# A graph-network kernel on one core: transposed z and score products in the first attention pass, one-source one-hots and PSUM weights in both

## The chip, the core and the metric

The kernel runs on one core of a Trainium2 chip. The time is device microseconds from the start to the end of one execution. Engines: PE (matrix products; PEld is its weight load), DVE (vector), ACT (scalar and activation), POOL (GpSimd, which here issues the indirect gathers) and SP (which issues other DMAs).

## The reference

Four graph layers one after another over 6250 nodes with 128 features and 100,000 edges, each followed by a residual addition and a layer norm. The change touches the two attention layers. The first (4 heads of 32) scores an edge by `att`, per head, on a leaky sum:

```python
e = jax.nn.leaky_relu(x_l[src] + x_r[dst], NEG_SLOPE)      # (edges, 4, 32)
logits = jnp.einsum('ehc,hc->eh', e, att)
p = jnp.exp(logits - m[dst])                               # m: maximum per target
alpha = p / (segment_sum(p, dst)[dst] + 1e-16)
out = segment_sum(x_l[src] * alpha[:, :, None], dst)
```

The third layer (8 heads of 16) scores by the dot product of a query and a key row; the rest is the same with the roles of source and target exchanged:

```python
att = jnp.sum(Qh * Kh, axis=-1)                            # (edges, 8)
alpha = segment_softmax(att, row, num_nodes)
out = segment_sum(Vh * alpha[:, :, None], row)
```

## The kernel before

The edges are sorted by target and by source, and padded with one edge per node to 832 tiles of 128 positions. Five passes gather over these tiles: the first attention pass (`l0`, up to 3592 us of the trace), a scalar-score pass (`l1`), the second attention pass (`l2`, `dot` is true, from 5172 us), and two sum passes (`l3a`, `l3b`). Each pass is a loop over 208 groups of G = 4 tiles. It ends with a barrier, and node steps lie between the passes, so that a pass overlaps with nothing else.

In a pass, POOL does only `gather_rows` (L938): four indirect gathers a group of 128 rows each, into a ring of 8 groups (`RING`). It goes on when the group that last used the buffer is done with it; in the attention passes that is `val_done` of seven groups before. SP loads the window of node rows of each tile (L1051) and the run masks (L1053), four and six groups ahead. ACT's queue loads the slot rows and stores the partial sums.

The engines run a software pipeline in the order in which the code lists it; step k of each loop works on several groups:
- PE: transpose of the scores of group k-2 (L1069), transpose of the weights of k-3 (L1074), z of k, sums of k-4 (L1093). In the first pass z is, for each tile, the one-hot `sel_t` as weights with the window rows streamed (L1084), plus the identity with the gathered rows (L1086). An f32 product is two instructions; so z is 16 and the sums are 8.
- ACT: relu of z of k (L1116, only `l0`), copy of the weights of k-3 from PSUM into `val` (L1122), copy of the sums of k-4 to SBUF (L1127), exp of k-2 (L1133).
- DVE: `sel_t` of k+1 (L1145), prefix scan of k-2 (L1151), leaky of k-1 (L1163; in `l2` the product of z and the rows, L1158), top scan of k-2 (L1167), `prod` = z times att of k-1 (L1172, only `l0`), `sel` of k-3 (L1178), diff of k-2 (L1184), the value multiplication `val` of k-3 (L1188), the reduction of `prod` to the scores of k-1 (L1195) and a small copy (L1199).

The same two instructions in both passes have two SBUF sources of full size, `sel` and `val`; in `l0` there is `prod` besides. The sum passes build their one-hots from one tensor and one per-partition scalar a tile (L1410, L1412).

## Time and profile before

| what | us |
|---|---|
| median of 3 runs | 9392.61 (9376.02 to 9402.11) |
| the profiled execution | 9417.1 |
| its span | 9415.4 |
| mean granted clock of PE | 0.704 of full |

Busy over the whole span: POOL 5483 us (58%), PE 4862 us (52%), DVE 4576 us (49%), ACT 1853 us (20%). No engine is busy all the time, because the kernel has stages with different limits; the busy share of each has to be read stage by stage. The clock is the one that the chip grants to PE; it has two levels, 0.50 and 1.00, and a mean between them is a mixture. An idle time is written with what ended it; "issue" means that the profile shows nothing that the engine waited for, and "remote" that the releaser is not known. Ends of PE's instructions are modelled.

### The profile page before, as it was taken

How to read it: one execution, taken by the hardware profiler on the slowest of the kernel's cores; microseconds unless marked ns; L12 is line 12 of the kernel's file. 1: busy time of each engine (PE TensorE's matmuls, PEld its weight loads, DVE VectorE, ACT ScalarE, POOL GpSimd, SP SyncE). 2: the span in 40 equal slices, each digit the busy share in tenths (PEclk: the TensorE clock that was granted, in tenths of full speed). 3: DMA queues.
4: the chain of work that ended last, by engine and by line, in shares of the span. 5: the costliest groups of instructions: out<-in, count | busy, mean ns of one | idle time of the engine just before them, and what ended most of it. 6: DMA issues, size and time to landing. Idle time of an engine off the chain costs nothing. (4 is left out here: it accounts for less than half of the span.)

```text
span 9415.4 us, 112649 instructions
## 1 busy us (share of the span) xinstructions
PE 4861.8 (52%) x32998; PEld 3933.7 (42%) x32998; DVE 4576.4 (49%) x15755; ACT 1853.2 (20%) x4001; POOL 5483.4 (58%) x5311
## 2 busy tenths in 40 slices
PE   2367776777666663566665544544333334422322
PEld 2144444444555553556563444443233333322221
DVE  8866666663766666223233556555444443211113
ACT  0023333322222223111112111111222222211100
POOL 0235555553767673666663777775566665566664
PEclk9878888886888886555556767777666667655555
DMA  0011111114555552455553667665244443233332
GB/s 17 1 34 35 35 34 34 35 29 114 152 140 148 146 148 63 104 117 119 117 119 101 191 182 198 189 188 145 78 140 138 139 139 115 77 93 93 94 89 75
DMA packets 1304018, 990.43 MB, mean 105 GB/s; under 512 B 287713, under 2 KB 1192995, under 8 KB 1303411
## 3 DMA queue, kind: packets, MB, share of 16 engines
q0 software_dynamic: 183088, 352.33, 14.8%
q1 hardware_dynamic: 700995, 378.63, 14.4%
q10 hardware_dynamic: 419328, 252.26, 10.0%
q8 instruction: 273, 4.47, 0.2%
q14 instruction: 334, 2.74, 0.1%
HBM read 613.75 MB, written 368.79 MB: 104 GB/s over the span
## 5 line engine op out<-in xcount | busy, mean ns | idle before, releaser
L938 POOL DMA_INDIRECT l_rows<-tab,by_src x1664 | 1769.4, 1063 | 902.5 <-issue 480.2
L670 POOL DMA_INDIRECT sorted_dst<-pay,place_i x783 | 832.9, 1064 | 809.3 <-DVE place_i L618 590.6
L938 POOL DMA_INDIRECT l_rows<-tab,by_dst x832 | 945.4, 1136 | 520.5 <-issue 232.8
L938 POOL DMA_INDIRECT l3a_rows<-tab,by_dst x832 | 802.7, 965 | 440.3 <-issue 222.9
L938 POOL DMA_INDIRECT l3b_rows<-tab,by_dst x832 | 797.5, 958 | 421.6 <-issue 241.8
L1385 PE MATMUL l3b_ps_o<-l3b_rows,l3b_sel 128*128 128x128 f32 x1664 | 353.2, 390 | 837.3 <-issue 436.9
L1084 PE MATMUL l_ps_z<-l_win,l_sel_t 128*128 128x128 f32 x3328 | 732.0, 344 | 59.7 <-issue 19.1
L1385 PEld LDWEIGHTS l3b_ps_o<-l3b_rows,l3b_sel 128*128 128x128 f32 x1664 | 317.0, 289 | 873.9 <-issue 487.9
L1412 DVE TENSOR_SCALAR l3b_sel<-iota,by_dst 128x128 f32<-128x128 f16 x832 | 182.8, 296 | 1005.0 <-DMA lo_rows<-low_rows 827.4
L1084 PEld LDWEIGHTS l_ps_z<-l_win,l_sel_t 128*128 128x128 f32 x3328 | 586.7, 242 | 80.5 <-issue 44.3
L1409 DVE TENSOR_SCALAR l3a_kind<-iota,etype_at 128x256 f16<-128x256 f16 x832 | 244.7, 294 | 707.1 <-DMA l_win<-win 559.1
L1382 PE MATMUL l3a_ps_c<-l3a_kind,l3a_sel 128*128 128x256 f16 x832 | 186.1, 368 | 740.9 <-DVE l3a_sel L1412 526.5
L1093 PE MATMUL l_ps_o<-l_val,l_sel 128*128 128x132 f32 (+1 forms) x3328 | 567.4, 326 | 0.0
L1258 PE MATMUL l_ps_x<-l_win,l_sel_t 128*128 128x4 f32 x1664 | 364.6, 342 | 379.2 <-DVE l_e L1311 358.1
L1258 PEld LDWEIGHTS l_ps_x<-l_win,l_sel_t 128*128 128x128 f32 x1664 | 377.7, 332 | 398.8 <-DVE l_sel_t L1305 382.6
L1093 PEld LDWEIGHTS l_ps_o<-l_val,l_sel 128*128 128x128 f32 x3328 | 533.4, 238 | 0.3
L1265 PE MATMUL l_ps_o<-l_rows,l_sel 128*128 128x132 f32 x1664 | 438.0, 444 | 94.8 <-issue 94.3
L1127 ACT ACTIVATE l_sums<-l_ps_o 128x528 f32<-128x528 f32 (+1 forms) x416 | 257.1, 618 | 1126.6 <-remote 602.6
L1188 DVE TENSOR_TENSOR l_val<-l_rows,l_val 128x512 f32<-128x512 f32 x416 | 283.8, 682 | 318.7 <-ACT l_val L1122 232.5
L1315 DVE TENSOR_SCALAR l_sel<-iota,by_src,l_weight 128x128 f32<-128x128 f16 x832 | 247.7, 352 | 384.3 <-PE l_ps_o L1265 253.1
L1069 PE MATMUL l_ps_s<-ident,l_score 128*16 128x128 f32 (+1 forms) x416 | 127.3, 306 | 587.7 <-issue 310.5
L1265 PEld LDWEIGHTS l_ps_o<-l_rows,l_sel 128*128 128x128 f32 x1664 | 383.8, 333 | 101.2 <-issue 100.0
(412 smaller groups left out, 12542.6 us busy)
## 6 DMA issues: line engine op xcount, KB each, us to landing
parts<-l_sums ACTq DMA_DIRECT2D x416, 264.0 KB
l_win<-win SPq DMA_DIRECT2D x1664, 64.0 KB
parts<-l3a_sums SPq DMA_DIRECT2D x208, 512.0 KB
l_row<-slot_rows ACTq DMA_DIRECT2D x624, 128.0 KB
parts<-l_sums ACTq DMA_DIRECT2D x208, 272.0 KB
parts<-l3b_sums SPq DMA_DIRECT2D x208, 256.0 KB
low_bc<-lo_rows SPq DMA_DIRECT2D x194, 256.0 KB
l_rows<-tab,by_src POOLq DMA_INDIRECT x1664
```

Source lines behind the costliest of these rows:

```text
L670: pool.indirect_dma_start(sorted_dst, bass.IndirectOffsetOnAxis(ap=place_i[:, 4 * DST + s % 4, g:g + 1], axis=0), pay[:, col(s, g), :], No ...
L938: pool.indirect_dma_start(rows[:, q, g, :], None, table, bass.IndirectOffsetOnAxis(ap=index[:, k * G + g:k * G + g + 1], axis=0))\
L1084: mm = pe.matmul(ps_z[k % 2][:, g], sel_t[:, k % 2, g], win[:, b, g], start=True, stop=dot)
L1093: mm = pe.matmul(ps_o[j % 2][:, g // 2, g % 2 * w:(g % 2 + 1) * w], sel[:, j % 3, g], val[:, j % 2, g], start=True, stop=True)
L1127: act.activation(sums[:, j % OB].rearrange("p (i g) w -> p i (g w)", i=2), ps_o[j % 2][:, :, 0:2 * w], ACT.Copy).then_inc(sums_done, 1)
L1188: dve.tensor_tensor(val[:, j % 2, :, 0:D].rearrange("p g (h d) -> p g h d", h=heads), rows[:, j % RING, :, v0:].rearrange("p g (h d) -> p ...
L1258: mm = pe.matmul(ps_x[k % 2][:, g], sel_t[:, k % 2, g], win[:, b, g], start=True, stop=True)
L1265: mm = pe.matmul(ps_o[j % 2][:, g // 2, g % 2 * w:(g % 2 + 1) * w], sel[:, j % 2, g], rows[:, j % RING, g], start=True, stop=True)
L1315: return dve.tensor_scalar(sel[:, j % 2, g], c.iota16[:, 0:P], real_slot[:, at:at + 1], weight[:, j % 2, g:g + 1], ALU.is_equal, ALU.mult)
L1382: pe.matmul(ps_c[k % 2][:, g], sel16[:, k % 2, g], kind[:, k % 2, g], start=True, stop=True)
L1385: mm = pe.matmul(ps_o[k % 2][:, g], sel[:, k % 2, g], rows[:, k % RING, g], start=True, stop=True)
L1409: dve.tensor_single_scalar(kind[:, k % 2, g], c.iota16[:], types[:, at:at + 1], ALU.is_equal)
```

## The change

In the first attention pass z is formed transposed: the window rows and the gathered rows are the weights, and `sel_t` and the identity are streamed. After relu and leaky, the scores come from four products with `att_cols` (for each of the four tiles a 128 x 16 tile with att's heads in their columns), accumulated in PSUM; `prod`, its reduction and the transpose of the scores are gone there. `load_weights` builds `att_cols`. In both passes `sel` is built by four instructions with one tensor and one scalar, `val` reads the weights from PSUM (`ps_p`) and not from the copy in `val`, the weight transpose waits for `val_done` in place of `weight_done`, and ACT copies the weights before relu.

```diff
@@ load_weights
-                 (c.att[:], spread(w["L0_gnn_att"].rearrange("h c -> (h c)"))),
+                 (att_col[:], w["L0_gnn_att"].rearrange("h (c a) -> (h c) a", a=1)),
...
+            dve.memset(c.att_cols[:], 0.0).then_inc(rel_zero, 1)
...
+            flat = c.att_cols[:].rearrange("p g h -> p (g h)")
+            for h in range(heads):
+                own = slice(h * (D // heads), (h + 1) * (D // heads))
+                dve.tensor_copy(flat[own, h::G * heads + heads], att_col[own, 0:1].to_broadcast([D // heads, G]))
@@ attention_pass, PE
-                    pe.wait_ge(score_done, j + 1)
                     wait_count(pe, diff_done, j)
-                    pe.transpose(ps_s, score[:, j % 2], c.ident[:]).then_inc(score_ps, 1)
+                    if dot:
+                        pe.wait_ge(score_done, j + 1)
+                        pe.transpose(ps_s, score[:, j % 2], c.ident[:]).then_inc(score_ps, 1)
+                    else:
+                        pe.wait_ge(leaky_done, j + 1)
+                        for g in range(G):
+                            mm = pe.matmul(ps_s, c.att_cols[:, g], z[:, j % 2, g * P:(g + 1) * P],
+                                           start=g == 0, stop=g == G - 1)
+                        mm.then_inc(score_ps, 1)
...
-                    wait_count(pe, weight_done, j)
+                    wait_count(pe, val_done, j)
...
-                        mm = pe.matmul(ps_z[k % 2][:, g], sel_t[:, k % 2, g], win[:, b, g], start=True, stop=dot)
-                        if not dot:
-                            mm = pe.matmul(ps_z[k % 2][:, g], c.ident[:], rows[:, q, g], start=False, stop=True)
+                        if dot:
+                            mm = pe.matmul(ps_z[k % 2][:, g], sel_t[:, k % 2, g], win[:, b, g], start=True, stop=True)
+                        else:
+                            pe.matmul(ps_z[k % 2][:, g], win[:, b, g], sel_t[:, k % 2, g], start=True, stop=False)
+                            mm = pe.matmul(ps_z[k % 2][:, g], rows[:, q, g], c.ident[:], start=False, stop=True)
@@ attention_pass, ACT
-                if k < GROUPS and not dot:
-                    act.wait_ge(z_done, k + 1)
-                    wait_count(act, prod_done, k - 1)
-                    act.activation(z[:, k % 2], ps_z[k % 2].rearrange("p g d -> p (g d)"), ACT.Relu, scale=1.0 - LEAK)\
-                       .then_inc(relu_done, 1)
                 if 0 <= k - 3 < GROUPS:
...
                     act.activation(val[:, j % 2, :, D:w], ps_p, ACT.Copy).then_inc(weight_done, 1)
+                if k < GROUPS and not dot:
+                    act.wait_ge(z_done, k + 1)
+                    wait_count(act, score_ps, k - 1)
+                    act.activation(z[:, k % 2], ps_z[k % 2].rearrange("p g d -> p (g d)"), ACT.Relu, scale=1.0 - LEAK)\
+                       .then_inc(relu_done, 1)
@@ attention_pass, DVE
-                if 0 <= k - 1 < GROUPS and not dot:
-                    j = k - 1
-                    dve.wait_ge(leaky_done, j + 1)
-                    dve.tensor_tensor(prod[:, j % 2].rearrange("p (g d) -> p g d", g=G),
-                                      z[:, j % 2].rearrange("p (g d) -> p g d", g=G),
-                                      replicate(c.att[:], 1, G), ALU.mult).then_inc(prod_done, 1)
...
-                    dve.tensor_tensor(sel[:, j % 3], replicate(c.iota16[:, 0:P], 1, G),
-                                      replicate(slot[:, j * G:j * G + G], 2, P), ALU.is_equal)
+                    for g in range(G):
+                        t = j * G + g
+                        dve.tensor_single_scalar(sel[:, j % 3, g], c.iota16[:, 0:P], slot[:, t:t + 1], ALU.is_equal)
...
-                                      replicate(val[:, j % 2, :, D:w], 3, width), ALU.mult).then_inc(val_done, 1)
-                if 0 <= k - 1 < GROUPS:
+                                      replicate(ps_p, 3, width), ALU.mult).then_inc(val_done, 1)
+                if 0 <= k - 1 < GROUPS and dot:
```

## Rows read from the trace of the kernel before

**Rows 1.** Busy time by engine in the five gather passes, in order of time
```profile
...
core 0: us, PE busy (x) PEld busy (x) DVE busy (x) ACT busy (x) POOL busy (x), PEclk, DMA share, GB/s
2225.00:3592.00 1367.00, 855.77 (x5408) 769.53 (x5408) 932.79 (x2100) 304.09 (x833) 944.65 (x832) 0.83 0.55 144
3786.00:4991.00 1205.00, 741.72 (x3264) 716.36 (x3264) 361.86 (x1647) 150.82 (x405) 803.27 (x832) 0.50 0.53 117
5172.00:6530.00 1358.00, 682.79 (x3740) 590.09 (x3741) 792.87 (x1878) 215.04 (x624) 965.55 (x832) 0.72 0.66 189
6703.00:7892.00 1189.00, 452.18 (x2424) 384.72 (x2424) 482.95 (x2447) 297.79 (x400) 802.36 (x832) 0.64 0.45 135
8088.00:9265.00 1177.00, 348.50 (x1640) 312.46 (x1640) 179.87 (x819) 118.80 (x203) 797.46 (x832) 0.57 0.34 92
```

**Rows 2.** Waits of the first pass: total us, times, longest us
```profile
...
POOL l_rows L938 <- issue: 232.8, 758, 0.8
DVE l_val L1188 <- ACT l_val L1122: 229.1, 130, 6.6
...
ACT l_sums L1127 <- remote: 185.3, 65, 13.6
POOL l_rows L938 <- DVE l_val L1188: 160.2, 73, 9.7
...
PE l_ps_z L1084 <- DMA l_rows<-tab,by_dst: 5.3, 4, 1.7
```

**Rows 3.** Instruction groups, first pass, 2600 to 3200: busy us, mean ns, idle before
```profile
...
L938 POOL DMA_INDIRECT l_rows<-tab,by_dst x372 | 416.0, 1118 | 185.3 <-issue 101.6 <-DVE l_val L1188 83.7
...
L1195 DVE TENSOR_REDUCE l_score<-l_prod 128x16 f32<-128x512 f32 x90 | 61.1, 679 | 0.0
L1178 DVE TENSOR_TENSOR l_sel<-iota,by_dst 128x512 f32<-128x512 f16 x90 | 60.5, 672 | 0.0
L1172 DVE TENSOR_TENSOR l_prod<-l_z,att 128x512 f32<-128x512 f32 x90 | 58.8, 654 | 0.0
```

**Rows 4.** Instruction groups of the third pass, 5500 to 6100 us
```profile
...
L938 POOL DMA_INDIRECT l_rows<-tab,by_src x372 | 436.4, 1173 | 160.8 <-issue 111.0 <-DVE l_val L1188 49.7
```

**Rows 5.** Instruction groups of the fourth pass, 6800 to 7880 us
```profile
...
L938 POOL DMA_INDIRECT l3a_rows<-tab,by_dst x757 | 727.4, 961 | 355.0 <-issue 201.3 <-DMA l_win<-win 139.4 <-PE l3a_ps_o L1385 14.3
...
L1412 DVE TENSOR_SCALAR l3a_sel<-iota,by_dst 128x128 f32<-128x128 f16 x760 | 225.9, 297 | 0.0
```

**Rows 6.** Order of time, first pass, half clock: start us, duration us, engine
```profile
...
2925.26 0.95 POOL L938 DMA_INDIRECT l_rows<-tab,by_dst  x1 [0.30 <-issue]
2925.37 0.65 DVE L1163 SCALAR_TENSOR_TENSOR l_z<-l_ps_z,l_z 128x512 f32<-128x512 f32 x1
...
2926.07 0.80 PE L1084 MATMUL l_ps_z<-l_win,l_sel_t 128*128 128x128 f32 x2
2926.28 0.65 DVE L1172 TENSOR_TENSOR l_prod<-l_z,att 128x512 f32<-128x512 f32 x1
...
2926.51 1.86 POOL L938 DMA_INDIRECT l_rows<-tab,by_dst  x1 [0.30 <-issue]
...
2926.87 0.67 DVE L1178 TENSOR_TENSOR l_sel<-iota,by_dst 128x512 f32<-128x512 f16 x1
...
2929.64 1.97 PE L1093 MATMUL l_ps_o<-l_val,l_sel 128*128 128x132 f32 x8
```

**Rows 7.** Order of time, the next group, full clock
```profile
...
2932.71 0.46 PE L1084 MATMUL l_ps_z<-l_win,l_sel_t 128*128 128x128 f32 x2
...
2934.57 1.07 PE L1093 MATMUL l_ps_o<-l_val,l_sel 128*128 128x132 f32 x8
...
2938.14 0.61 ACT L1127 ACTIVATE l_sums<-l_ps_o 128x528 f32<-128x528 f32 x1 [2.70 <-remote]
```

**Rows 8.** Busy time in three us of each of these two groups
```profile
...
2926.00:2929.00 3.00, 3.00 (x14) 2.96 (x15) 1.74 (x5) 0.00 (x0) 2.39 (x3) 0.50 0.54 163
2933.00:2936.00 3.00, 2.63 (x24) 2.44 (x22) 2.49 (x6) 0.67 (x2) 2.39 (x3) 1.00 0.73 182
```

More of the change, by code:

```diff
@@ L678, in load_weights @@
         kit = Kit(nc, st)
-        att_cols = kit.sb("att_cols", [P, 2])
+        att_cols, att_col = kit.sb("att_cols", [P, 2]), kit.sb("att_col", [P, 1])
         kernel_t = kit.sb("kernel_t", [P, P])
@@ L768, in _ @@
             dve.wait_ge(turned, 4)
-            dve.wait_ge(rel_zero, 1)
+            dve.wait_ge(rel_zero, 2)
+            heads = 4
+            flat = c.att_cols[:].rearrange("p g h -> p (g h)")
+            for h in range(heads):
+                own = slice(h * (D // heads), (h + 1) * (D // heads))
+                dve.tensor_copy(flat[own, h::G * heads + heads], att_col[own, 0:1].to_broadcast([D // heads, G]))
             dve.tensor_copy(c.rel_w[:, 0], ps_rw[:, 0]).then_inc(copied, 1)
@@ L1957, in build @@
         c.w3 = kit.sb("w3", [P, 2, 3 * D])
-        c.gamma, c.beta, c.att = (kit.sb(n, [P, D]) for n in ("gamma", "beta", "att"))
+        c.gamma, c.beta = (kit.sb(n, [P, D]) for n in ("gamma", "beta"))
+        c.att_cols = kit.sb("att_heads", [P, G, G * 4])
         c.rel_w = kit.sb("rel_w", [P, 2, 2, D])
```

## The prediction

> **What bounds the kernel now.** I read first the table of the five gather passes [rows 1]: each is a loop of 208 groups with four gathers a group issued by POOL, 832 in all, and nothing of one pass overlaps the next. The change touches the first (from 2225 us) and the third (from 5172 us). The reader should compare the POOL column with the span. The three passes that are left alone take 1205, 1189 and 1177 us with POOL busy for 803, 802 and 797 us. The two that change take 1367 and 1358 us with POOL busy for 945 and 966 us, for the same 832 gathers. What the other engines do differs by far more (PE busy 856 us in the first pass and 349 us in the last) and moves the span less.
>
> Second, the waits of the first pass [rows 2]: between gathers POOL needs 233 us in small pieces of 0.3 us (issue), and 160 us for the value multiplication to free a buffer. PE waits for gathered rows only 5 us. So POOL is occupied for 945 + 233 = 1178 of 1367 us and the rest, 189 us, are stretches in which the ring of eight groups is full. The same subtraction with 0.3 us per gather (250 us) leaves 152, 137 and 130 us in the three other passes and 142 us in the third. The remainder hardly depends on what is computed; the POOL term does.
>
> Third, why a gather takes longer in the two passes. Its mean is 1118 and 1173 ns [rows 3, 4] against 961 ns [rows 5]. In the order of time [rows 6] a gather that starts at 2925.26 beside the leaky step, which reads PSUM and SBUF, takes 0.95 us; the one at 2926.51, beside prod (z and att, both SBUF) and then sel (iota and slot, both SBUF), takes 1.86 us and goes on till the end of the stretch of both. So a DVE instruction with two SBUF sources holds POOL's gather up; one with a PSUM source does not. The rows of the one-hots in the fourth pass, tensor against one scalar, stand beside gathers of 961 ns [rows 5]: those don't either.
>
> Fourth, PE. Its clock alternates between half (0.50, 1.2 GHz) and full (1.00, 2.4 GHz) [rows 8]. At half clock the eight z products take from 2926.07 to 2929.64, 3.57 us, and the sums 1.97 us; at full clock 1.86 and 1.07 us [rows 6, 7]. After the full-clock sums ACT still waits 2.70 us and the profile names no releaser; in the whole pass such waits are 185 us, up to 13.6 us long [rows 2, 7].
>
> **The change part by part.** *The two-source instructions go.* First pass: prod (654 ns), the reduction (679 ns) and the 672 ns sel go [rows 3]; the value multiplication keeps its size but reads the weights from PSUM; four one-source one-hots of about 297 ns come [rows 5]. DVE: -0.65 - 0.68 - 0.67 + 1.19 = -0.8 us a group, but it was busy only 933 of 1367 us, so this gives nothing by itself. POOL loses all its two-source partners but one, the top scan, which I take as harmless. Bound from the other passes: 945 - 803 = 142 down to 945 - 797 = 147 us saved, and nothing if the new one-hots hold gathers up too. I take 141 us, by the nearest pass in PE work. Third pass: 966 - 803 = 162 to 168 us, again nothing at the other end; I take 162 us.
>
> The Trainium skill, page "SBUF — State Buffer", section "Who interferes with whom", says that GpSimd shares one pair of ports with VectorE, and that a VectorE instruction with two SBUF inputs contends with GpSimd's reads; the lengthened gathers agree. It also says that tensor_scalar can enter a mode that uses both ports and then contends as well, which speaks against this change. By that rule the four one-hots could hold POOL for as long as the sel they replace, and the gain would be little or none; the fourth pass's 961 ns beside twelve such instructions a group does not show it [rows 5].
>
> *The one-hots in the third pass* cost DVE 4 x 0.297 - 0.65 = about 0.5 us a group, 112 us of busy time on top of 793 of 1358 us [rows 1]. They lie before diff, exp and the weight transpose. Hidden by POOL's pace it is nothing, wholly exposed 112 us; DVE stays below 80% of the new span, so I take 12 us.
>
> *PE in the first pass* loses one transpose of the scores and gains four products a group, each with a 16-column weight tile and 128 streamed columns. The nearest rows are the z products: 1.86/8 = 0.23 us at full and 3.57/8 = 0.45 us at half clock, so at most 0.9 and 1.8 us a group. Swapping weights and streamed operand of the z products leaves sixteen passes of 128 columns: nothing. At full clock PE needs 1.86 + 1.07 + 0.9 + 0.3 = 4.1 us, which lies under POOL's 4 x (0.965 + 0.30) = 5.06 us. At half clock it needs 3.57 + 1.97 + 1.8 + 0.3 = 7.6 us, and now a group at half clock takes 6.64 us from z to z [rows 6, 7]. A mean clock of 0.83 [rows 1] means 34% of the time at half clock: of some 1225 us that is 417 us or 55 groups, each 1.0 us longer, 55 us. The ring of eight groups and the earlier scores cover part: between 0 and 55, and below nothing if the earlier products keep the clock up; I take 20 us.
>
> *Order and waits.* The score products now wait for the leaky step instead of the reduction, an instruction earlier on DVE. ACT copies the weights before relu instead of after it, so that the value multiplication no longer waits for the z products: that wait is 229 us now, in 130 groups [rows 2]. It is a shorter way around the loop, but POOL sets the pace, so I count it only as what keeps PE's addition cheap. The weight transpose now waits for the value multiplication of the group before. Behind it on PE stand the z products and the sums, and ACT's relu waits for those. In the third pass PE has by then waited for a reduction that DVE does after that same multiplication: nothing. In the first it costs nothing as long as DVE runs ahead; if not, up to the 0.7 us of a value multiplication a group, 140 us. The loads of the start (a 128-value column in place of a broadcast, one memset, four small copies) are within 2 us and I take nothing.
>
> **Sum.** First pass -141 + 20 = -121 us; third pass -162 + 12 = -150 us; together -271 us. The profiled execution took 9417.1 us (span 9415.4), so 9146 us for it. The median of the runs shown is 9392.6 us, 24.5 us less, and the predicted time is 9392.6 - 271 = 9122 us.
>
> **The rivals.**
> *The first pass is PE-bound, the third gains.* All 55 us of PE and the 2.70 us waits stay, the way around the loop (z, sums, wait, ACT's sums and exp, weight transpose) remains the limit, and what POOL saves turns into waiting for the value multiplication. For it: PE waited for gathered rows 5 us only. Against: the remainder of 189 us is little more than the 130 to 152 us of passes with far lighter loops. First pass 0, third -150: 9243 us. Chance 0.16.
>
> *The one-hots hold POOL too* (the change does not do what it says; also the page's tensor_scalar rule). Then a gather stays at 1.12 to 1.17 us, and the extra DVE work is even: 9393 us, within 25. Against: 961 ns [rows 5]. Chance 0.07.
>
> *Slower: PE stays at half clock.* The second pass runs at 0.50 throughout although PE is busy 742 of 1205 us [rows 1]. If the first pass did the same, a group would need 7.6 us of PE, and adding the remainder common to all passes, 130/208 = 0.6 us, 8.2 us: 208 x 8.2 = 1706 us, +339. With -150 in the third, 9582 us. It decides as soon as a group of the first pass averages above 6.57 + 150/208 = 7.3 us. Against: the z products, which make the larger part of PE's work, are the same as now and had 0.83. Chance 0.06.
>
> *The stretches shrink as well.* The shorter way around the loop removes the excess of the first pass's remainder, 189 - 130 = about 60 us, and PE costs nothing: -141 - 60 - 162 = -363, 9030 us. Chance 0.13.
>
> **How the numbers follow.** The forecast, 9122 us, has 0.58; its own range is 9050 to 9220, by the ends of PE's 0 to 55 and DVE's 0 to 112 us. About 0.3% (28 us) is what a measurement of this kernel can tell from no change. The range that should hold the time 8 times in 10 takes in the forecast, most of the PE-bound case and the near side of the last one: 9040 to 9290. Faster: 0.58 + 0.16 + 0.13 = 0.87, less 0.02 for a PE-bound case that eats the third pass's gain: 0.85. Same: 0.08. Slower: 0.07.
>
> **What would show it.** The gathers of both passes at 0.95 to 0.97 us mean and POOL busy about 800 us in each; spans near 1245 and 1210 us. If the gathers shorten and the first pass's span does not, with POOL waiting for the value multiplication for over 250 us, PE or the loop was the bound. If the gathers stay above 1.1 us, the port argument is wrong. A mean clock of the first pass below 0.7 would make the slower case true. In the third pass DVE busy near 900 us is the price of the one-hots.

## The result, and the profile after

The changed kernel takes 9680.2 us (median of 4 runs, 9677.0 to 9696.1); the kernel before, run beside it, 9384.4 us. The ratio is 1.0333, with a 95% interval of 1.0311 to 1.0354: 296 us slower where the forecast was 271 us faster. The profiled execution took 9678.6 us, span 9676.8 us.

The table of the changed kernel by stretch, in the columns of [rows 1]; the first and the third line are the passes that change:

```profile
core 0: us, PE busy (x) PEld busy (x) DVE busy (x) ACT busy (x) POOL busy (x), PEclk, DMA share, GB/s
2202.00:3726.00 1524.00, 1019.34 (x6864) 909.80 (x6864) 722.54 (x2310) 328.01 (x833) 813.67 (x832) 0.82 0.49 130
3916.00:5121.00 1205.00, 740.52 (x3259) 715.26 (x3259) 360.29 (x1648) 150.66 (x405) 800.25 (x832) 0.50 0.53 117
5303.00:6790.00 1487.00, 758.21 (x3738) 658.86 (x3739) 829.95 (x2502) 210.51 (x624) 805.88 (x832) 0.69 0.60 172
6964.00:8156.00 1192.00, 448.71 (x2436) 383.06 (x2436) 481.85 (x2461) 298.88 (x403) 801.25 (x832) 0.65 0.45 135
8350.00:9527.00 1177.00, 341.21 (x1632) 305.94 (x1632) 179.23 (x814) 118.00 (x202) 794.83 (x832) 0.57 0.34 92
```

POOL's busy time fell as forecast, from 945 to 814 us and from 966 to 806 us, and yet the passes grew, from 1367 to 1524 us and from 1358 to 1487 us (157 + 129 = 286 of the 296 us). The three other passes are as they were. The gathers in the instruction groups of the changed kernel's first pass (busy us, mean ns | idle before):

```profile
L944 POOL DMA_INDIRECT l_rows<-tab,by_dst x832 | 814.0, 978 | 778.4 <-DVE l_val L1198 460.7 <-issue 219.8 <-POOLq L789 97.9
```

A gather takes 978 ns, near the 961 ns of [rows 5]. But POOL now waits 461 us for the value multiplication, where it waited 160 us [rows 2]. The waits of the changed kernel (total us, times, longest us), first pass:

```profile
DVE l_prefix L1166 <- remote: 474.3, 95, 8.3
POOL l_rows L944 <- DVE l_val L1198: 460.7, 122, 8.6
...
ACT l_sums L1142 <- remote: 257.2, 75, 6.7
ACT l_z L1136 <- remote: 236.7, 46, 26.4
```

and third pass:

```profile
ACT l_sums L1142 <- remote: 723.8, 89, 12.0
...
POOL l_rows L944 <- DVE l_val L1198: 421.9, 93, 9.3
```

"remote" means that the profile names no releaser. Each of these three instructions reads what PE has just put into PSUM: the scores, the sums, z. Two of them wait for a transfer as well (the sums for an earlier store, the scan for the run masks), but the trace's records of signals decide it: each of these waits ends at a signal that only PE gives, recorded over 1.5 us after the modelled end of the products that give it (for the sums at a median of 6.0 us, for the scores 6.0 us, for z 3.0 us). Whether the result or only its signal is late, they don't show. In the first pass ACT's wait for the sums grew from 185 [rows 2] to 257 us; the two others stood in the kernel before at:

```profile
DVE l_prefix L1151 <- remote: 59.1, 14, 11.8
ACT l_z L1116 <- remote: 150.6, 25, 10.5
```

The order of time of one such stretch, changed kernel (start us, duration us, engine, idle before):

```profile
3016.76 0.83 DVE L1189 TENSOR_SCALAR l_sel<-iota,by_dst 128x128 f32<-128x128 f16 x4
...
3017.43 0.39 PE L1101 MATMUL l_ps_z<-ident,l_rows 128*128 128x128 f32 x2
...
3017.66 1.07 PE L1108 MATMUL l_ps_o<-l_val,l_sel 128*128 128x132 f32 x8
...
3018.61 0.95 POOL L944 DMA_INDIRECT l_rows<-tab,by_dst  x1 [0.30 <-issue]
3018.65 1.05 PE L1080 MATMUL l_ps_s<-l_z,att_heads 128*16 128x128 f32 x8
...
3020.38 0.60 ACT L1136 ACTIVATE l_z<-l_ps_z 128x512 f32<-128x512 f32 x1 [4.31 <-remote]
3020.46 0.60 DVE L1160 TENSOR_SCALAR l_sel_t<-l_row,lane 128x512 f32<-128x512 f16 x1 [1.99 <-remote]
3020.52 4.14 SPq L1057 DMA_DIRECT2D l_win<-win  x4
...
3023.63 0.95 POOL L944 DMA_INDIRECT l_rows<-tab,by_dst  x1 [0.30 <-issue]
3024.70 0.61 ACT L1142 ACTIVATE l_sums<-l_ps_o 128x528 f32<-128x528 f32 x1 [3.71 <-remote]
...
3026.44 0.41 DVE L1166 TENSOR_TENSOR_SCAN l_prefix<-l_run,l_ps_s 16x128 f32<-16x128 f32 x1 [5.39 <-remote]
...
3029.59 0.95 POOL L944 DMA_INDIRECT l_rows<-tab,by_dst  x1 [5.02 <-DVE l_val L1198]
```

The z products end at 3017.82 as the profile models them, and the three instructions that wait for them on three engines (relu on ACT, the next `sel_t` on DVE, the next window on SP) start within 0.14 us of each other, from 3020.38 on. The sums' matmuls end at 3018.73, the score products at 3019.70; their readers start at 3024.70 and 3026.44. In between POOL issues gather after gather, one each 1.25 us. Then the ring is full, and POOL stands for 5.02 us until the loop that it ran ahead of has freed a buffer. The hold of the two-source instructions is gone, and a later result takes its place.

The passes that the change leaves alone have such waits too. In the last one POOL waits for the sums of PE alone (`sums_ps`); the label names an old transfer with the same signal number, but the signal that ends these waits is again PE's:

```profile
POOL l3b_rows L944 <- DMA lo_rows<-low_rows: 136.5, 36, 7.2
```

### The profile page after: what moved, and what is told of

It is laid out like the page before. It is cut to its first block and busy times, and to the rows that moved or that the text cites. A ratio compares the mean times of both kernels' runs of the same rounds, so it can differ in the third digit from the quotient of the medians.

```text
span 9676.8 us, 116192 instructions
## 1 busy us (share of the span) xinstructions
PE 5066.9 (52%) x34454; PEld 4125.2 (43%) x34454; DVE 4396.7 (45%) x16592; ACT 1870.6 (19%) x4001; POOL 5184.2 (54%) x5311
## 5 line engine op out<-in xcount | busy, mean ns | idle before, releaser
L944 POOL DMA_INDIRECT l_rows<-tab,by_src x1664 | 1606.6, 966 | 1194.8 <-issue 464.7
L944 POOL DMA_INDIRECT l_rows<-tab,by_dst x832 | 814.0, 978 | 778.4 <-DVE l_val L1198 460.7
L1166 DVE TENSOR_TENSOR_SCAN l_prefix<-l_run,l_ps_s 16x128 f32<-16x128 f32 (+1 forms) x416 | 169.6, 408 | 1095.4 <-remote 474.3
L1087 PE MATMUL l_ps_p<-ident,l_weight 16*128 16x16 f32 (+1 forms) x416 | 110.9, 267 | 1031.7 <-ACT l_weight L1148 768.1
L1108 PE MATMUL l_ps_o<-l_val,l_sel 128*128 128x132 f32 (+1 forms) x3328 | 600.0, 339 | 0.1
L1108 PEld LDWEIGHTS l_ps_o<-l_val,l_sel 128*128 128x128 f32 x3328 | 566.0, 251 | 0.5 <-DVE l_val L1198 0.3
L1087 PEld LDWEIGHTS l_ps_p<-ident,l_weight 16*128 16x128 f32 (+1 forms) x416 | 64.3, 155 | 1152.8 <-ACT l_weight L1148 824.3
L1392 PEld LDWEIGHTS l3a_ps_c<-l3a_kind,l3a_sel 128*128 128x128 f16 x832 | 90.9, 125 | 802.2 <-DVE l3a_sel L1422 563.9
L1100 PE MATMUL l_ps_z<-l_sel_t,l_win 128*128 128x128 f32 x1664 | 419.1, 342 | 20.4 <-DVE l_sel_t L1160 16.7
```

The costliest lines, as they stand in the source:

```text
L944: pool.indirect_dma_start(rows[:, q, g, :], None, table, bass.IndirectOffsetOnAxis(ap=index[:, k * G + g:k * G + g + 1], axis=0))\
L1087: pe.transpose(ps_p.rearrange("p g h -> p (g h)"), weight[:, j % 2], c.ident[0:hg, 0:hg])\
L1100: pe.matmul(ps_z[k % 2][:, g], win[:, b, g], sel_t[:, k % 2, g], start=True, stop=False)
L1108: mm = pe.matmul(ps_o[j % 2][:, g // 2, g % 2 * w:(g % 2 + 1) * w], sel[:, j % 3, g], val[:, j % 2, g], start=True, stop=True)
L1392: pe.matmul(ps_c[k % 2][:, g], sel16[:, k % 2, g], kind[:, k % 2, g], start=True, stop=True)
```

## The experiments

How a line is read below: *pass* is the time from the start of the first to the start of the last gather, slightly shorter than the stretches above; *gather* is the mean of one; *stalls* are POOL's pauses of over 0.8 us in the pass. For comparison, the kernel before: first pass 1337 us, gather 1.136 us, stalls 155 us; third pass 1330, 1.161, 118. The change: 1494, 0.978, 463; 1459, 0.969, 423. A pass repeats less well than the whole: the same code took 1376, 1377 and 1388 us in the third pass of three kernels, and 1501 and 1469 us in the first pass of one; differences under some 30 us in one pass are not read. All of these have the three other passes at 1170 to 1220 us; a second kind of session, with those at 1045 to 1059 us, comes after it.

### One hold at a time

*The change, with the one-hots of all four groups in one two-source instruction again.*

```
-                    for g in range(G):
-                        t = j * G + g
-                        dve.tensor_single_scalar(sel[:, j % 3, g], c.iota16[:, 0:P], slot[:, t:t + 1], ALU.is_equal)
+                    dve.tensor_tensor(sel[:, j % 3], replicate(c.iota16[:, 0:P], 1, G),
+                                      replicate(slot[:, j * G:j * G + G], 2, P), ALU.is_equal)
```

> The changed kernel with one part undone: sel is again one instruction with two SBUF sources. Theory A (the holds helped): the gathers that DVE held up gave PE's results room to come out; with sel back, a gather is about 1.05 us again on the mean, both passes shorten by 60 to 100 us against the changed kernel, about 9530 us in all. Theory B (plain cost): the third pass lost by the 0.5 us of the four one-hots and returns to 1358 us, the first pass stays at about 1520 us because its loss is PE's added products: about 9550 us, with the first pass unchanged as the mark that tells it from A.

Measured 9548.5 us, 1.0175 (1.0088 to 1.0263) of the kernel before (9380.1 us beside it). Passes 1449 (gather 1.030, stalls 365) and 1376 (1.005, 309). The first pass is 45 us shorter than the change's and not unchanged, which speaks for theory A, though for less than its 60.

*The change, with the value weights read from SBUF again.*

```
-                                      replicate(ps_p, 3, width), ALU.mult).then_inc(val_done, 1)
+                                      replicate(val[:, j % 2, :, D:w], 3, width), ALU.mult).then_inc(val_done, 1)
```

> The changed kernel with one part undone: the value multiplication reads the weights from their SBUF copy. Theory A (the holds helped): gathers lengthen by about 0.1 us, both passes shorten by 40 to 80 us, about 9560 us. Theory B (plain cost): the source of the weights costs nothing either way, 9680 us within 20.

Measured 9497.8 us, 1.0133 (1.0096 to 1.0169). Passes 1405 (1.049, 309) and 1359 (1.050, 249). Both put a source of hold back, both make gathers longer, and both make the kernel faster than the change, by 132 and 182 us (theory B had 9680 for the second).

*The kernel before, with the one-source one-hots alone* (the first diff, turned round).

> The kernel before with one part done: sel by four one-source instructions. Theory A (the holds helped): gathers near 1.02 us, both passes longer by 50 to 100 us with POOL's waits for the value multiplication up by as much as the gathers shrink and more, about 9540 us. Theory B (plain cost): 0.5 us of DVE a group matters only where DVE is in the loop: the third pass longer by 110 to 128 us, the first by less than 40, about 9510 us.

Measured 9558.1 us, 1.0186 (1.0066 to 1.0306). Passes 1501 (0.984, 467) and 1339 (1.047, 232). Its first pass in the table by stretch:

```profile
2211.00:3740.00 1529.00, 910.60 (x5371) 821.72 (x5371) 955.61 (x2698) 302.60 (x823) 818.43 (x832) 0.79 0.49 128
```

and in the list of waits:

```profile
POOL l_rows L938 <- DVE l_val L1189: 469.3, 134, 8.5
ACT l_sums L1127 <- remote: 392.3, 96, 7.9
DVE l_prefix L1151 <- remote: 258.8, 67, 6.2
```

This kernel has none of the new PE work, and its first pass is as long as the change's, with the same picture. So the loss does not need the added products. It does not follow that they are free: with the one-hots undone in the change, the first pass stayed at 1449 us, 112 above the kernel before. The third pass fits neither theory: it lost 95 us of POOL's busy time and is 9 us longer, where A had 50 to 100 and B 110 to 128.

*The kernel before, with the value weights read from PSUM alone*, and the weight transpose behind the value multiplication, as that needs.

```
-                    wait_count(pe, weight_done, j)
+                    wait_count(pe, val_done, j)
-                                      replicate(val[:, j % 2, :, D:w], 3, width), ALU.mult).then_inc(val_done, 1)
+                                      replicate(ps_p, 3, width), ALU.mult).then_inc(val_done, 1)
```

> The kernel before with one part done: the value multiplication reads the weights from PSUM, and the weight transpose waits for it. Theory A (the holds helped): both passes longer by 20 to 60 us, about 9460 us. Theory B (plain cost): no change in the third pass, where PE had waited for a later step anyway, and at most 20 us in the first: 9385 to 9405 us.

Measured 9488.1 us, 1.0111 (1.0024 to 1.0198). Passes 1349 (1.132, 171) and 1377 (1.008, 308). In the first pass nearly nothing changes, hold included; in the third the hold goes and the stalls come. Alone the two edits cost 178 and 108 us, together 286, about the whole change's 296. By pass they don't add up: 164 + 12 us in the first, where the change has 157, and 9 + 47 in the third, where it has 129.

*The same two again, in another session, beside the kernel before itself*, since two of these intervals are wide.

> The kernel before, profiled beside the others. If the light passes take about 1050 us: gathers of 1.15 to 1.2 us in the two attention passes, 4 x (1.17 + 0.25) = 5.7 us a group, about 1190 us a pass, no wait without a releaser, 8098 us. If they take 1170 us or more: as at first, 9390 us within 150.

> The kernel before with sel by four one-source instructions. Theory E, light passes of about 1050 us: POOL sets the pace, the gathers shorten by 0.08 to 0.14 us and each attention pass by 60 to 110 us: about 7940 us. Light passes of 1170 us or more: 1.5 to 2% slower than before, as b_sel_one.

> The kernel before with the value weights read from PSUM. Theory E, light passes of about 1050 us: gathers shorter by up to 0.15 us in the third pass, hardly in the first, together 50 to 130 us faster: about 8010 us. Light passes of 1170 us or more: about 1% slower than before, as b_val_psum.

Measured 1.0012 (0.9997 to 1.0026) for the kernel against itself, 1.0152 (1.0035 to 1.0269) for the one-hots (9547.7 against 9381.5 us) and 1.0096 (1.0079 to 1.0113) for the value weights. Passes 1469 and 1362, and 1345 and 1388. It repeats: + 166 and + 93 us. Beside the 1352 and 1338 us of the kernel before, run beside them, the one-hots cost the first pass 117 and the third 24 us, the value weights nothing in the first and 50 in the third.

*The new z and PE products alone*: the change with both of the first two diffs.

> The first pass's part alone: transposed z, scores from PE products, order and waits as in the changed kernel; sel with two SBUF sources and the value weights from their SBUF copy as in the kernel before. Theory A (the holds decide): prod's hold of 0.1 us a gather goes, so the first pass is 20 to 60 us longer; the third pass equals before within 15 us: about 9420 us. Theory B (plain cost of PE's products): the first pass longer by 100 us or more, 9490 us.

Measured 9631.9 us, 1.0123 (1.0024 to 1.0223) of a kernel before that took 9514.5 us beside it. First pass 1439 with stalls of only 162, but with POOL busy for 1034 us, more than the 945 before. In the order of time:

```profile
2909.26 0.65 DVE L1187 TENSOR_TENSOR l_sel<-iota,by_dst 128x512 f32<-128x512 f16 x1
2909.46 2.08 POOL L944 DMA_INDIRECT l_rows<-tab,by_dst  x1 [0.30 <-issue]
...
2910.04 0.67 DVE L1197 TENSOR_TENSOR l_val<-l_rows,l_val 128x512 f32<-128x512 f32 x1
```

The earlier weights let the value multiplication follow the one-hots at once, so one gather is held by both. This kernel is slow because of the hold, as the prediction's picture has it, and the price is the opposite of what the change pays. It isn't an isolated price of the products, as I had meant it to be: at this ratio it would take 9500 us beside a kernel before of 9384, theory B's number, but with POOL's hold for its reason.

Its third pass says something else. It differs from the kernel before by one wait alone, that of the weight transpose for the value multiplication; both two-source instructions are there. Yet POOL is busy 879 us instead of 966, its stalls are 262 instead of 118, and the pass takes 1376 us, 46 more, where at most 15 were expected (the slower session makes some 15 of them, by its other passes of 1218, 1199 and 1182 us). So the wait costs by itself, and less hold can also be the result of more stalls, and not only their cause.

### Pauses in POOL, and the ring

*The change, with POOL filling an unused tile after each group of four gathers.*

```
+                wait_count(pool, idled, k)
+                pool.memset(idle[:], 0.0).then_inc(idled, 1)
```

> The changed kernel, with a fill of a 128x768 scratch tile by POOL after each group's four gathers in the two attention passes, 0.7 to 0.8 us a group (128x128 fills start 0.14 us apart at the kernel's start). Theory A (any break in POOL's gathers lets PE's results out): both passes shorten by 80 to 130 us against the changed kernel, about 9470 us, although POOL does more. Theory C (what helped was something of DVE's two-source instructions other than the break): POOL's fill comes out of its waits for buffers, no pass is shorter: 9680 us or up to 50 more.

Measured 9613.4 us, 1.0104 (0.9971 to 1.0237) of 9514.5 us: about 220 us less than the change's 1.0333 would give (the low end of one interval and the high end of the other leave about 70 us; the two ratios come from two sessions), with more work. The fill in the groups of the whole span:

```profile
L1070 POOL MEMSET l_idle<- 128x768 f32 x416 | 314.5, 756 | 0.2
```

The third pass in the table by stretch, the fills among POOL's 968 us:

```profile
5337.00:6738.00 1401.00, 770.40 (x3727) 672.47 (x3727) 918.25 (x2498) 209.53 (x621) 968.28 (x1040) 0.68 0.64 183
```

315 us of idle work were put into POOL; the third pass is 1371 us (gather 0.976), 88 us less than the change's, and the first 1448 us, 46 us less, though even the kernel before, run beside it, took 1.4% longer than beside the change. The stalls fall to 259 and 191 us. The gathers are as many and as short; spaced, they cost less. The third pass meets theory A's 80 to 130 us, the first stays below them.

*Fewer groups ahead*: the ring keeps its eight buffers, but POOL may fill only six (first and second pass), five (third) and four (last two). Once in the change, once in the kernel before.

```
-    wait_count(pool, used, k - RING + 1)
+    wait_count(pool, used, k - ahead + 1)
```

> The changed kernel with POOL allowed fewer groups ahead, by a lower count in its wait alone: 6 in the first and second pass, 5 in the third, 4 in the two sum passes, where it was 8. Theory A (unbroken gathers delay PE's results): POOL stops after fewer gathers in a row, so each pass is shorter, the attention passes by 30 to 100 us each and the sum passes by 20 to 60. Theory D (the ring's depth is what carries the loop over the late results): fewer groups ahead make every pass longer, the attention passes by 50 us or more each.

> The kernel before with the same lower counts. Theory A (unbroken gathers delay PE's results): sum passes shorter by 20 to 60 us each, attention passes by 0 to 60, because DVE's holds break the gathers already: about 9300 us. Theory D (the ring's depth carries the loop): every pass longer, 9450 us or more.

Measured 1.0307 (1.0215 to 1.0398) and 0.9983 (0.9953 to 1.0012): in the change as slow as it is (passes 1527 and 1527), in the kernel before nothing (1379 and 1345), and the other passes stay at 1182 to 1220 us, as in the kernel with the fills beside them. Neither theory's number came: no pass got shorter, and only the change's third pass, 68 us longer (some 15 of them the session's), has what theory D gives. So a shorter lead, and with it a shorter unbroken run of gathers, takes nothing of the loss away.

### The same kernels in another kind of session

The next four kernels ran in a session where the kernel before took 8098.1 us, 14% less, with no edit of it.

> The kernel before with POOL's fill of a 128x768 scratch tile after each group's gathers in the two attention passes. Theory A (any break in POOL's gathers lets PE's results out, and DVE's holds, 0.7 us a group, do already what the fill does): little is left to gain, between 40 us faster and 60 us slower. If instead breaks simply add up, both passes shorten by 50 us or more each, down to the 1180 to 1200 us of the light passes.

> The changed kernel with the same length of fill cut in four, one of 128x192 after each gather. Theory A with the length of unbroken gathers as what counts: shorter pieces of POOL's work help as much or more than one break a group, 9470 us or less beside a kernel before of 9385. If the sum of the breaks or a break of at least some length counts: less than a_pause gave, 9550 to 9680 us.

(*b_pause*: the fill in the kernel before. *a_pause_each*: a fill of 192 values a partition after each single gather of the change.)

*Each gather brings 4 of a row's 128 values, as many gathers as before* (the text on record says what its output lacks):

```
+        pool.indirect_dma_start(rows[:, q, g, 0:4], None, table.rearrange("n (a b) -> (n a) b", b=4),
```

> The changed kernel in whose two attention passes each gather fetches 16 bytes a row in place of 512 or 1024 (the rest of the rows is a constant: the attention outputs are not the reference's). POOL issues as many gathers of 128 rows. If PE's late results come from the traffic of the gathers, both passes run at the pace of POOL, 5.1 us a group or 1070 to 1100 us each, and the waits without a named releaser nearly vanish. If they come from POOL's own work of issuing, the passes stay within 60 us of 1494 and 1459 us.

*One gather a group instead of four, in both attention passes of the change:*

```
-    for g in range(G):
-        pool.indirect_dma_start(rows[:, q, g, :], ...
+    pool.indirect_dma_start(rows[:, q, 0, :], ...
-                        pe.wait_ge(landed[q], landed_before[q] + 16 * G * (k // RING + 1))
+                        pe.wait_ge(landed[q], landed_before[q] + 16 * (k // RING + 1))
```

> The changed kernel in whose two attention passes only the first of the four gathers of a group is issued (the other rows are a constant: the attention outputs are not the reference's). It shows the loop's own pace. Theory A (POOL's gathers delay PE's results): 4.2 to 4.8 us a group, 870 to 1000 us a pass, and waits without a named releaser near nothing. Theory B (the loop is slow by itself, by PE's added work and its clock): the passes stay above 1350 us.

Measured, against 8098.1 us: the kernel before with fills 8363.8 us, 1.0322 (1.0282 to 1.0363), passes 1392 and 1348, POOL busy 1013 us with the gathers of the first and nowhere a stall, so that its fills are added work (266 us for some 315 of fills). The change with small fills 0.9949 (0.9928 to 0.9969), passes 1207 and 1235. The thin gathers 0.9640 (0.9612 to 0.9668), passes 1075 and 1112. One gather in four 0.8966 (0.8940 to 0.8992), passes 820 and 796 us: the loop without POOL's pace takes 3.9 us a group, less than the 4.2 to 4.8 expected. Nothing could be concluded on the loss, since it wasn't known whether it is there at all in such a session. So the unchanged change ran next, beside a repetition as a link to that session:

> The changed kernel once more. Theory E (two conditions): where the light passes take about 1050 us and no wait is without a releaser, POOL sets the pace and the two attention passes come down to 5.1 to 5.3 us a group, 1060 to 1100 us each, 3 to 4% faster than the kernel before beside it; where the light passes take 1170 us or more, it is 3% slower as at first. Theory B (plain cost of the change): slower by 1 to 3% in either.

> The changed kernel in whose two attention passes only the first of the four gathers of a group is issued (the other rows are a constant, so the attention outputs are not the reference's), once more. Where the light passes take about 1050 us: 820 and 796 us a pass as before. Where they take 1170 us or more: if POOL's gathers cause PE's late results, 820 to 900 us a pass and few waits without a releaser in the two; if something else causes them, 1000 us or more a pass, with those waits still there.

Measured 7797.6 us against 8098.5 us: 0.9627 (0.9608 to 0.9646). Here the same change is 301 us faster. The repetition gave 0.8974 (0.8952 to 0.8996), as before. The first and the third pass of the change there, in the table by stretch:

```profile
1623.00:2728.00 1105.00, 902.69 (x6872) 796.21 (x6872) 725.29 (x2315) 332.02 (x835) 825.29 (x837) 0.94 0.72 179
4102.00:5246.00 1144.00, 696.70 (x3752) 599.22 (x3752) 840.95 (x2507) 222.70 (x627) 867.07 (x838) 0.76 0.78 225
```

Its waits in the first pass:

```profile
POOL l_rows L944 <- issue: 245.1, 804, 0.3
...
PE l_ps_z L1100 <- DMA l_rows<-tab,by_dst: 181.6, 145, 3.7
```

and in the third:

```profile
DVE l_prod L1173 <- DMA l_rows<-tab,by_src: 252.2, 131, 5.8
```

POOL is busy in the first pass for about what it was in the other session (825 and 814 us; in the third 867 and 806), but no wait without a releaser is left in the first pass, POOL's waits for the value multiplication are gone (in the third pass 15 us are left, in pieces of 0.3 us), and now PE and DVE wait for gathered rows. POOL alone makes 825 + 245 = 1070 of the 1105 us. It is what the prediction described, but for one thing: the remainder is gone as well. In the kernel before, in the first kind of session, POOL's stalls are 155, 169, 118, 149 and 134 us in the five passes, in the change 463, 172, 423, 150 and 134; here POOL has no pause of over 0.8 us in any of the five. Its wait for PE in the last pass, 136.5 us above, has become:

```profile
POOL l3b_rows L944 <- PE l3b_ps_o L1395: 0.6, 2, 0.3
```

The two kinds of session part at one place. POOL's first indirect transfer comes at 392 us. The changed kernel in the first kind, its first 392 us and 966 us of the sort's scatters:

```profile
0.00:392.00 392.00, 109.74 (x1603) 82.09 (x1603) 363.12 (x1800) 3.67 (x5) 6.12 (x34) 1.00 0.04 11
534.00:1500.00 966.00, 686.24 (x7761) 454.16 (x7759) 598.86 (x2082) 299.52 (x480) 508.85 (x480) 0.83 0.14 34
```

The same kernel in the second kind, stretches of the same lengths:

```profile
0.00:392.00 392.00, 109.67 (x1603) 82.12 (x1603) 363.26 (x1801) 3.67 (x5) 6.12 (x34) 1.00 0.04 11
495.00:1461.00 966.00, 860.63 (x12301) 609.24 (x12302) 942.09 (x3287) 473.11 (x759) 742.65 (x733) 1.00 0.22 54
```

The first 392 us agree to a quarter of a microsecond in every column, so it isn't the speed at which the engines work by themselves. From the scatters on, the first kind gets 480 of them done in the time in which the second gets 733. Of the waits of that stretch in the first kind, one of ACT for PE's products again has no releaser:

```profile
ACT lo L412 <- remote: 287.4, 47, 9.6
```

*Fewer gathers in the first kind*: the kernel before, with one gather a group in the first pass alone.

> The kernel before in whose first attention pass only the first of the four gathers of a group is issued (the other rows are a constant, so the output is not the reference's); its third pass is as before. Light passes of 1170 us or more: if POOL's gathers cause PE's late results, the first pass runs at the loop's own pace of 4.6 us a group, 960 us, with few waits without a releaser; if not, it stays above 1200 us. Light passes of about 1050 us: the first pass 900 to 960 us, the third 1150 to 1200 us, its gathers 1.16 to 1.2 us.

Measured 8972.6 us, 0.9529 (0.9501 to 0.9557) of 9418.4 us. It fell in the first kind of session: from first to last gather its last pass takes 1175 us (the stretch of 1200 below takes in what follows), and its third 1325, as ever. The first and the last pass in the table by stretch:

```profile
2213.00:3140.00 927.00, 679.97 (x5268) 609.58 (x5268) 889.87 (x2043) 298.29 (x808) 198.85 (x208) 0.99 0.63 165
7650.00:8850.00 1200.00, 352.92 (x1664) 316.03 (x1664) 183.00 (x832) 121.58 (x208) 802.98 (x840) 0.57 0.35 92
```

and the waits of the first pass:

```profile
POOL l_rows L946 <- DVE l_val L1200: 716.9, 199, 11.3
ACT l_z L1128 <- PE l_ps_z L1098: 571.4, 203, 5.5
...
ACT l_sums L1139 <- PE l_ps_o L1105: 47.0, 200, 1.0
```

Every wait for PE names PE's own instruction again, and the one for the sums is never over 1.0 us (it was up to 13.6 us [rows 2]). The second pass of the same execution, untouched, keeps its late results (ACT's wait for its sums: 566 us without a releaser). So they go with POOL's gathers: gone at a quarter of them, there at four a group; rates in between were not tried. POOL's long wait here is what one gather a group leaves over.

## Why the prediction was wrong

*What sets POOL's busy time: right.* The gathers came to 978 and 969 ns and POOL to 814 and 806 us; 0.95 to 0.97 us and about 800 us were forecast. (One row was misread: the gather of 1.86 us does not go on till the end of prod and sel, 2927.54, but 0.83 us beyond it [rows 6].) Undoing either part brought some of the hold back, and each time the gather's mean rose (1.030 and 1.049 us).

*The one-hots hold POOL too: wrong, as given.* The Trainium skill, page "SBUF — State Buffer", section "Who interferes with whom", lets tensor_scalar take both ports in its 2-port modes. No hold as long as the instruction shows here; a small one does: the changed kernel's gathers with no DVE instruction beside them take 0.951 us, the 125 of the first pass beside the one-source `sel_t` alone 0.992 on the mean and up to 1.21 us. Its other rule, that two SBUF inputs of VectorE contend with GpSimd, agrees with the gather of 2.08 us above.

*PE's added products, + 20 us: neither confirmed nor refuted.* The one-hots without them gave 1501 and 1469 us for the first pass, the change 1494; no kernel has the products without either the hold or the late results. The clock was 0.82 (0.83 before), so the slower rival with PE at half clock did not occur; the loss has another mechanism, although that rival alone had the right direction.

*The one-hots in the third pass, + 12 us on DVE: too dear a price on DVE, and the wrong place.* DVE was busy for 830 us, not 900: four one-hots take 0.83 us together in the order of time, not 4 x 0.297.

*The wait of the weight transpose: counted at nothing in the third pass.* The value weights from PSUM lengthened that pass from 1330 to 1377 and 1388 us. There the hold's removal and the wait came together. The kernel with the new products alone has in that pass nothing but the wait, and took 1376 us, some 30 more than before if its slower session is allowed for (an estimate from its other passes). Beside one-source one-hots the same wait made 1359 against 1339 and 1362 us. So the wait's share lies between nothing and two thirds.

*The step that failed* is "The remainder hardly depends on what is computed; the POOL term does", and with it the terms of - 141 and - 162 us, which took the whole saving of POOL to be time of the pass. I had it from five passes whose remainders were 130 to 189 us (189 with 233 us for the pieces between gathers, but the others with 250; by the same 250 the first has 172). The remainder rose instead: POOL's stalls from 155 to 463 us and from 118 to 423 us. Spans of 1245 and 1210 us were forecast, 1524 and 1487 came.

Two readings went wrong in it. The first: in the first pass PE waited 5 us for gathered rows, so hardly anything waited for POOL, and POOL itself stood for a full ring. There, time saved on POOL adds to the time that it stands. The prediction has this number, but gives the case 0.16. In the third pass of the kernel before something did wait for POOL, and in the change it no longer does:

```profile
DVE l_prod L1158 <- DMA l_rows<-tab,by_src: 103.7, 41, 4.8
```

The second: the remainder is itself made of PE's late results, and what the change does to them was no term of the sum. By the trace's records of signals (some are missing, so the sums are rough), the waits that a signal of PE ended over 1.5 us after PE's modelled end add up, over all engines, to 395 us in the first pass before and 1210 after, and to 813 and 1302 in the third. In the passes left alone they are the same before and after (1182 and 1188, 1308 and 1316, 1817 and 1820 us), and in the second kind of session there are none in the five passes of the change.

The first rival (PE-bound) named the mark that came true, POOL waiting over 250 us for the value multiplication, but it priced the first pass at 0 and left the third its gain. It lacked that PE's results themselves come later when the gathers follow each other unheld. The trace of before held the sign, the waits without a releaser, up to 13.6 us [rows 2, 7]; I listed them and gave them no price. The range of the forecast was also too narrow by its own terms: PE's 0 to 55 and DVE's 0 to 112 us give 9090 to 9257, not 9050 to 9220; 9680 lies outside both.

The kernels of one hold at a time say it together. Hold is here POOL's busy time above 795 us, that of the lightest pass; then the length of the pass:

| kernel | first pass: hold, length | third pass: hold, length |
|---|---|---|
| before | 150, 1337 | 171, 1330 |
| before, value weights from PSUM | 147, 1349 | 44, 1377 |
| before, one-source one-hots | 23, 1501 | 76, 1339 |
| change, value weights from SBUF | 78, 1405 | 79, 1359 |
| change, two-source one-hots | 62, 1449 | 41, 1376 |
| change | 19, 1494 | 11, 1459 |
| change, both undone (session 1.4% slower) | 239, 1439 | 84, 1376 |

The first pass lost its hold, and its time, with the one-hots, the third more with the value weights and their wait. Over both, 131 + 160 us of hold removed came with 157 + 129 us of pass. Down to a hold of some 80 us little is lost in the third pass (9 to 46 us), and the largest losses, 129 to 164 us (117 in the repetition), stand where it is nearly gone. The last row shows the other end: too much hold costs as well. The hold is not turned by hand, though; a pass with more stalls has fewer gathers to hold, as the wait alone showed. What does not depend on that is the fill, which spaces the gathers without touching DVE and recovered a part, and the one gather a group, at which the late results are gone. These show that the rush of gathers costs time in this kind of session; by what way a gather makes PE's results late is not shown.

*The sizes.* In the second kind of session, where this delay is absent, the change gave - 301 us, forecast - 271. The direction and the mechanism are the forecast's, but the nearness is partly luck: the spans were 1105 and 1144 us against 1245 and 1210, and the kernel before was not profiled there, so that the two passes' shares can't be checked.

*What stays open.* What makes the two kinds of session differ: chip, time or load. The runs' records number the chips, and the same number stands beside a session of each kind, but whether it names the same chip isn't known. Also whether the issue of gathers or their traffic delays PE's results: one gather in four takes both away, and the thin gathers ran only in the second kind, where there is nothing to remove. The transfers themselves need no more of the DMA engines in the first kind: 0.49 of 1524 us and 0.72 of 1105 us, 747 and 796 us, for the same 198 MB. No kernel here beats the kernel before in the first kind of session; in the second the change itself is the best that computes everything.

## What to carry to other kernels

Before an engine's saving is counted as time of a pass, look whether anything waits for that engine; if it is the one that stands for a free buffer, something else sets the pace. A wait that the profile leaves without a releaser is a price to be put into the sum, with a case of its own. An instruction that is held up also spaces what follows it: ask what comes late when it comes in a rush, and try the removal by itself, and a deliberate pause, before building on it. And a ratio holds for the kind of session it was measured in: look at an untouched stage of the kernel in both runs (here the last passes, 1177 or 1049 us) before comparing two sessions.

## What the runs showed of the hardware

- In one kind of session ACT and DVE wait up to 26.4 us for a signal of PE (in the stretch shown they read the sums 6.0 us after the matmuls' modelled end) while POOL issues one indirect gather of 128 rows each 1.25 us. With a quarter of the gathers these waits are gone from the same pass of the kernel before (927 us instead of 1367).
- The profile can name a wrong releaser for such a wait: 136.5 us of POOL's waits for PE's sums stand under a transfer of the sort, `DMA lo_rows<-low_rows`.
- One program ran in 9380 to 9514 us in some sessions and in 8098 us in others. Of the changed kernel, profiled in both, the first 392 us are the same, and the difference comes after the first indirect transfers. The same edit was 3.3% slower in the first and 3.7% faster in the second.
- Two two-source DVE instructions one behind the other hold one gather for both: 2.08 us for 0.95 us.
- Filling POOL with 315 us of idle work over both passes made the changed kernel's third pass 88 us shorter, in the kind of session with the late results.
